# A graph kernel's count matrix: ScalarE's one-hots for two steps at once, a tile's normalization over several steps

## What is computed

```python
def _L0_gnn_ref(x, W_in, b_in, W_agg, W_self, b_hid, W_out, b_out, edge_index):
    ...
    h = x @ W_in + b_in
    deg = jax.ops.segment_sum(jnp.ones_like(dst, dtype=h.dtype), dst, num_segments=n)
    deg = jnp.maximum(deg, 1.0)[:, None]
    for l in range(n_layers):
        agg = jax.ops.segment_sum(h[src], dst, num_segments=n) / deg
        h = jax.nn.relu(agg @ W_agg[l] + h @ W_self[l] + b_hid[l])
    return h @ W_out + b_out
...
    edge_index = jnp.stack([src, dst])
    h = jnp.maximum(_layernorm(x, axis=-1), 0.0)
    x = x + _L0_gnn_ref(h, L0_gnn_W_in, L0_gnn_b_in, L0_gnn_W_agg, L0_gnn_W_self, L0_gnn_b_hid, L0_gnn_W_out, L0_gnn_b_out, edge_index)
```

## Time and profile before

| | us |
|---|---|
| median of 3 runs | 8374.22 |
| lowest, highest | 8368.79, 8376.52 |
| the profiled execution | 8375.02 |
| its span | 8373.1 |

### The profile page before, as it was taken

How to read it: one execution, slowest core, us unless ns; L and a number is a source line. 1 busy time by engine, 2 the same in 40 slices (tenths; PEclk the granted TensorE clock), 3 DMA queues, 4 the chain that set the end, 5 groups by cost and what they waited for, 6 DMA issues and landing times.

```text
span 8373.1 us, 125097 instructions
## 1 busy us (share of the span) xinstructions
PE 6630.0 (79%) x29456; PEld 4904.3 (59%) x29457; DVE 3788.5 (45%) x11036; ACT 2673.4 (32%) x7377; POOL 2390.8 (29%) x3589
## 2 busy tenths in 40 slices
PE   1666666669999999999688886479989996766766
PEld 0222222238887877777455554368778885666665
DVE  4888888851111111222477777512222333444443
ACT  0888888850000000111122221312223333222222
POOL 1111111110001001111577774000011114666664
PEclk9888888879999999999688887789999997888888
DMA  3444444467788778777233333388887773333332
GB/s 86 160 168 160 163 165 162 166 231 279 274 313 286 276 275 325 256 251 248 76 106 106 106 106 96 120 308 298 294 323 247 245 244 97 104 103 102 102 104 75
DMA packets 661157, 1591.43 MB, mean 190 GB/s; under 512 B 84103, under 2 KB 299160, under 8 KB 660825
## 3 DMA queue, kind: packets, MB, share of 16 engines
q1 hardware_dynamic: 534441, 1221.78, 41.1%
q0 software_dynamic: 126512, 366.84, 14.9%
HBM read 1199.09 MB, written 395.63 MB: 190 GB/s over the span
## 4 chain that ended last, share of the span: by engine, by line
PE 36%; issue 4%; DVEq 4%; DVE 4%; DMA 2%; ACT 1%; POOL 0%; SPq 0%; ACTq 0%; POOLq 0%
PE psum L1071 12%; PE psum L1211 6%; PE psum L1307 5%; PE psum L1277 3%; DVEq L2038 3%; PE psum L1199 2%; PE psum L1187 1%; PE psum L1289 1%; PE psum L1031 1%; PE psum L943 1%; PE psum L1040 1%; DMA slab<-adj 1%; DMA g_own<-own_dram 1%; DMA rb<-res 1%; PE psum L948 1%
## 5 line engine op out<-in xcount | busy, mean ns | idle before, releaser
L1071 PE MATMUL psum<-X,slab 128*128 128x512 f32 x12495 | 3115.2, 403 | 172.9 <-DMA slab<-adj 137.8
L1071 PEld LDWEIGHTS psum<-X,slab 128*128 128x128 f32 x12495 | 2350.7, 191 | 711.1 <-DMA slab<-adj 120.5
L1151 PE MATMUL psum<-hot_j,hot_key 128*128 128x392 bf16 x2348 | 692.3, 382 | 508.5 <-ACT hot_key L1409 426.6
L2035 DVE TENSOR_TENSOR acc<-acc,psum 128x264 f32 (+1 forms) x1660 | 699.6, 421 | 665.1 <-PE psum L1307 397.0
L1391 ACT ACTIVATE key_sq<-iota_row,edge_key 128x128 f32<-128x128 f32 x2348 | 813.7, 394 | 120.4 <-DVE staged L1859 2.3
L1914 DVE SCALAR_TENSOR_TENSOR staged<-staged,keep_all,psum 128x392 fp32r<-128x392 f32 x1174 | 727.3, 620 | 258.4 <-PE psum L1151 226.5
L1151 PEld LDWEIGHTS psum<-hot_j,hot_key 128*128 128x128 bf16 x2348 | 155.0, 102 | 987.0 <-ACT hot_key L1409 782.9
L794 POOL DMA_DIRECT2D table<-s_tab x147 | 80.2, 546 | 2048.8 <-DVE s_tab L1882 2048.8
L763 POOL TENSOR_TENSOR ends_fold<-fold,ends_all 128x16 fp32r<-128x16 f32 x1174 | 269.0, 229 | 1351.5 <-PE psum L1161 1328.3
L1161 PE MATMUL psum<-staged,ends_fold 128*16 128x392 f32 x1174 | 649.8, 553 | 0.5 <-DVE staged L1914 0.4
L1899 DVE TENSOR_SCALAR hot_j<-iota_j,edge_col 128x392 bf16<-128x392 bf16 x2348 | 643.2, 316 | 3.4
(11 more groups left out here) (351 smaller groups left out, 8374.6 us busy)
## 6 DMA issues: line engine op xcount, KB each, us to landing
slab<-adj SPq DMA_DIRECT2D x385, 1344.0 KB, 6.3
slab<-adj SPq DMA_DIRECT2D x315, 896.0 KB, 5.7
adj<-staged SPq DMA_DIRECT2D x1174, 196.0 KB, 1.9
X<-table SPq DMA_DIRECT2D x35, 1792.0 KB, 14.3
table<-s_tab POOLq DMA_DIRECT2D x147, 256.0 KB, 2.8
g_own<-own_dram POOLq DMA_DIRECT2D x35, 896.0 KB, 8.1
own_dram<-s_out POOLq DMA_DIRECT2D x147, 128.0 KB, 5.2
table<-s_tab SPq DMA_DIRECT2D x49, 256.0 KB, 2.1
```

The source lines that it names most:

```text
L1071: last = nc.tensor.matmul(sums_of(j), slab[:, c % SLABS, u, j * P:(j + 1) * P], X[:, d, :], start=(d == 0), stop=(d == KT - 1))
L1151: last = nc.tensor.matmul(psum[:, s % 4, 0:J], hot_key[:, s % 4, h, :], hot_j[:, s % 4, h, :], start=(h == 0), stop=(h == 1))
L2035: V.tensor_tensor(a, a, psum[:, bank, 0:w], ALU.add).then_inc(sem("summed"), 1)
```

## The change

ScalarE works in pairs of steps. `key_squares(t, m)` issues the four squares of steps 2m and 2m + 1 into one of three buffers, and one instruction of 512 columns writes `hot_key` of both steps into one of four buffers of two steps each. The squares of pair m + 1 now wait for the `hot_key` of pair m - 2, not for the instruction just ahead of them. `hot_key` of pair m waits for the product of step 2m - 7.

The stages get other places. VectorE: statistics at step 0, their merging (`in_moments`) at 1, the variance (`in_variance`) at 2, the reciprocal (`in_scale`) at 6, `nmr` (`in_shift`) at 7, `in_h0` at 12 (was 8), `in_rows` at 20 (was 15); the three waits for an own result that `then` made turn into waits one step later. ScalarE, in pairs: `in_sd` at pair 2, step 4 (was step 1), `in_h` at pair 4, step 8 (was 3), the copies at pairs 5 and 8, steps 10 and 16 (were 5 and 11), `in_hi` at pair 9, step 18 (was 13). TensorE: T1, P1, T2, P2 with P3 at 8, 10, 14, 16 (were 4, 6, 10, 12). SyncE: the load of the next tile at 10 (was 9), the tile's stores at 21 (was 20).

```diff
-                hot_key = sb("hot_key", [P, 4, 2, P], BF16, scope=late)
+                hot_key = sb("hot_key", [P, 4, 2, 2, P], BF16, scope=late)
...
-                key_sq = sb("key_sq", [P, 2, 2, P], scope=late)
+                key_sq = sb("key_sq", [P, 3, 2, 2, P], scope=late)
...
-                    if s == 9 and not (isinstance(t, int) and t == T - 1):
+                    if s == 10 and not (isinstance(t, int) and t == T - 1):
...
-                    if s == 20:
+                    if s == 21:
...
-                stages = {4: in_T1, 6: in_P1, 10: in_T2, 12: in_P2}
+                stages = {8: in_T1, 10: in_P1, 14: in_T2, 16: in_P2}
...
-                    pe.wait_ge(*ev("hot_key", t * BUILD + (s + 1)))
+                    pe.wait_ge(*ev("hot_key", t * (BUILD // 2) + (s // 2 + 1)))
...
-            def key_squares(t, s):
-
-                for h in range(2):
-                    last = nc.scalar.activation(key_sq[:, s % 2, h, :], iota_row[:], ACT.Square, bias=edge_key[:, h, bass.ds(t * BUILD + s, 1)],
-                                                scale=-1.0)
+            def key_squares(t, m):
+
+                for s in range(2 * m, 2 * m + 2):
+                    for h in range(2):
+                        last = nc.scalar.activation(key_sq[:, m % 3, s % 2, h, :], iota_row[:], ACT.Square,
+                                                    bias=edge_key[:, h, bass.ds(t * BUILD + s, 1)], scale=-1.0)
                 last.then_inc(sem("key_sq"), 1)
 
             def build(t, steps):
-                stages = {1: in_sd, 3: in_h, 5: taken_T("in", "T1", PS2_IN, ("P3", 1)), 11: taken_T("in", "T2", PS2_IN, ("P1", 2)), 13: in_hi}
-                for s in range(steps):
-                    n, static = t * BUILD + s, isinstance(t, int)
-                    if s in stages:
-                        stages[s](t)
-                    if not static or n + 1 < MEETS:
-                        if not static or n >= 1:
-                            act.wait_ge(*ev("hot_key", n))
-                        key_squares(t, s + 1)
-
-                    act.wait_ge(*ev("key_sq", t * BUILD + (s + 1)))
+                stages = {2: in_sd, 4: in_h, 5: taken_T("in", "T1", PS2_IN, ("P3", 1)), 8: taken_T("in", "T2", PS2_IN, ("P1", 2)), 9: in_hi}
+                for m in range(steps // 2):
+                    n, static = t * (BUILD // 2) + m, isinstance(t, int)
+                    if m in stages:
+                        stages[m](t)
+                    if not static or n + 1 < MEETS // 2:
+                        if not static or n >= 2:
+                            act.wait_ge(*ev("hot_key", t * (BUILD // 2) + (m - 1)))
+                        key_squares(t, m + 1)
+
+                    act.wait_ge(*ev("key_sq", t * (BUILD // 2) + (m + 1)))
                     if not static or n >= 4:
-                        act.wait_ge(*ev("meet_mm", t * BUILD + (s - 3)))
-                    nc.scalar.activation(hot_key[:, s % 4, :, :], key_sq[:, s % 2, :, :], ACT.Relu, bias=ones[:, 0:1], scale=-2.0).then_inc(sem("hot_key"), 1)
+                        act.wait_ge(*ev("meet_mm", t * BUILD + (2 * m - 6)))
+                    nc.scalar.activation(hot_key[:, m % 4, :, :, :], key_sq[:, m % 3, :, :, :], ACT.Relu, bias=ones[:, 0:1],
+                                         scale=-2.0).then_inc(sem("hot_key"), 1)
...
             def in_stats(t):
                 dve.wait_ge(*ev("in_x", t * 16 + 16))
                 V.memset(carrier[:, 6:7], 0.0)
-                then(V.bn_stats(st[:, 0, :], s_res[:, 0, :]), "in_st", t + 2)
+                V.bn_stats(st[:, 0, :], s_res[:, 0, :]).then_inc(sem("in_st"), 1)
+
+            def in_moments(t):
+                dve.wait_ge(*ev("in_st", t + 2))
                 V.memset(carrier[:, 6:7], 0.0)
-                then(V.bn_aggr(mv[:, 0, :], st[:, 0, :]), "in_mv", t + 2)
+                V.bn_aggr(mv[:, 0, :], st[:, 0, :]).then_inc(sem("in_mv"), 1)
+
+            def in_variance(t):
+                dve.wait_ge(*ev("in_mv", t + 2))
                 V.tensor_scalar_add(mv[:, 0, 1:2], mv[:, 0, 1:2], LN_EPS).then_inc(sem("in_ve"), 1)
 
-            def in_norm(t):
+            def in_scale(t):
                 dve.wait_ge(*ev("in_sd", t + 2))
-                then(V.reciprocal(rstd[:, 0:1], sd[:, 0:1]), "in_rstd", t + 2)
+                V.reciprocal(rstd[:, 0:1], sd[:, 0:1]).then_inc(sem("in_rstd"), 1)
+
+            def in_shift(t):
+                dve.wait_ge(*ev("in_rstd", t + 2))
...
-                stages = {0: in_stats, 2: in_norm, 8: in_h0, 15: in_rows}
+                stages = {0: in_stats, 1: in_moments, 2: in_variance, 6: in_scale, 7: in_shift, 12: in_h0, 20: in_rows}
```

More of the change, by code:

```diff
@@ L525, in build @@
         BUILD = 24
-        assert BUILD % AT_ONCE == 0 and (T - 1) * BUILD <= MEETS <= T * BUILD
+        assert BUILD % AT_ONCE == 0 and BUILD % 6 == 0 and MEETS % 2 == 0 and (T - 1) * BUILD <= MEETS <= T * BUILD
         def by_meets(eng, turn):
@@ L1150, in build @@
                     for h in range(2):
-                        last = nc.tensor.matmul(psum[:, s % 4, 0:J], hot_key[:, s % 4, h, :], hot_j[:, s % 4, h, :], start=(h == 0), stop=(h == 1))
+                        last = nc.tensor.matmul(psum[:, s % 4, 0:J], hot_key[:, s // 2 % 4, s % 2, h, :], hot_j[:, s % 4, h, :], start=(h == 0), stop=(h == 1))
                     last.then_inc(sem("meet_mm"), 1)
```

## The result

The changed kernel takes **8222.3 us** (median; 8214.1 to 8230.6), the kernel before 8373.1 us in the same comparison (8368.8 to 8376.5). The ratio is 0.982, with a 95% interval of 0.9803 to 0.9837. That is 151 us less. The prediction said 8240 us, 8160 to 8330, and faster with a chance of 0.91: it was right, 18 us too high.

The account below looks back on a forecast made before the run. ScalarE at 1.22 us a step heads the chain in the build; then VectorE's 25.9 us plus waits 0.39, 1.85, 0.3 and three quarters of 2.0 make 29.9 a tile, 2.75 less, times 48.9 = 134 us: 8240 us, range 8160 to 8330.

Parts of the forecast that it names:

- ScalarE's pace: A pair of steps on ScalarE costs 1.81 us (1.60 to 2.00), so ScalarE stops being the pace.
- Rival (4): Pairing does not free ScalarE, a pair costing 2.6 us: 8374 us stays; chance 0.03, shared with a balance of both.
- VectorE's own work: 24.0 us of steps plus 1.87 of stage operations, 25.9 us a tile; spreading the stages saves 0.36.
- Wait B: VectorE at step 8, as ScalarE's `in_h` waits for `nmr` from step 7: 1.85 us a tile, 0.36 more at low clock.
- three quarters: Share taken of the 2.0 us a tile that a low clock from Wait B until P1 would add.
- Wait A: VectorE at step 4, as ScalarE's `in_sd` waits for `in_variance` from step 2: 0.39 us a tile.
- Wait C: VectorE at step 10, behind P1 on TensorE: 1.63 us at the low clock, nothing at the high one.
- Wait D: VectorE at step 16, as P2 and P3 hold TensorE for 1.73 us: 0.3 us a tile.
- The sum: A build tile takes 28.4 us at high clock, 30.4 with it low until P1; 29.9 taken, 134 us less in all.
- Rival (1): The clock does not fall in Wait B: 28.4 us a tile, 8166 us; chance 0.18 for 8150 to 8200.
- Rival (2): The clock falls in every tile, back by P1's end: 30.4 us a tile, 8264 us; chance 0.64 together with the forecast.
- Rival (3): The clock stays low far beyond P1 and TensorE becomes the bound: 35.8 us a tile, 8529 us; chance 0.06.

Follow-up runs that it names:

- The fastest version: Changed kernel with VectorE's reciprocal at step 5, `nmr` at 6, bias at 14, ScalarE's stages one pair later, TensorE's two steps later: 8050.0 us, ratio 0.9615.
- waits filled: Changed kernel plus matmul products nobody reads on TensorE at step 4 and around T1 at step 8: ratio 0.9758 to the kernel before, tile 28.18 us.

## Why the prediction was right

**ScalarE's pace.** Right: a pair costs 1.78 us (1.81 predicted), `hot_key` 0.71 (0.70), its time on the engine 0.61 or 0.62 (0.61, by the copies of the earlier trace rows). Rival (4), that pairing frees nothing, is refuted by that.

**VectorE's own work.** The sum was near, two of its terms were not. In the changed kernel the statistics lengthen a step by 0.33 us (the `staged` at 1117.76 and 1119.09), `in_moments` and `in_variance` by 0.07 and 0.06, the reciprocal by 0.06 and `nmr` by 0.07. That is 0.59 for what was 1.21, so the spreading saves 0.62 us of work in this tile and not 3 x 0.12 = 0.36; it lies above the bound of 0.5. The term was made from the start of one small operation to the start of the next (0.46 where 0.34 would do), and left out that the next full operation, `hot_j`, is also held back after the last of a chain (1122.63 to 1122.85 is 0.22, and 0.06 now). With three additions of 0.33 the own work is 24.0 + 0.59 + 1.0 = 25.6 us and not 25.9. The fastest version, which hardly waits, shows it directly: 25.81 less 12.5/48.9 = 0.26 is 25.55.

**Wait B** was sized rightly. 1.85 was predicted at the high level, and the one filled with products is 1.82; 1.85 + 0.36 was predicted at the low one, and it is 2.08. That it is *the* new cost, and comes from where `nmr` stands, was shown by moving that line: 2.6 us a tile, C included. Over the 49 tiles its mean is 1.94 us, for the 1.85 and three quarters of 0.36, 2.12, that the sum of the prediction holds.

**Wait A** was 0.39 at the high level; it is 0.26 there (waits filled) and 0.60 in the tile shown, 0.43 in the mean. What the prediction missed is that the clock falls in A too: ScalarE's 2.76 us before `sd` leave TensorE 1.67 us idle. The sentence that ScalarE's waits are "harmless except behind B" is thereby wrong. With B gone and A left the tile takes 26.81 us and the clock is 0.91; with both gone 25.81 and 1.00.

**Wait C** was over-sized, 1.63 against 1.12 in the tile shown and 1.14 in the mean of the 37 tiles that have it. The step of TensorE at the low level was taken as 1.15 us. But those 1.15 were the rhythm of the keys, which ScalarE then made one every 1.22 us. In the trace of the kernel before, the key of the second of these steps ends at 1124.75 + 0.49 = 1125.24, and the weight load that needs it has waited 0.70 us for it:

```profile
1124.75 0.49 ACT L1409 ACTIVATE hot_key<-key_sq,ones 128x256 bf16<-128x256 f32 x1
...
1125.30 0.13 PEld L1151 LDWEIGHTS psum<-hot_j,hot_key 128*128 128x128 bf16 x2 [0.70 <-ACT hot_key L1409]
```

It is not what TensorE needs: with the keys ready it makes a step every 0.97 us (1122.93 to 1123.90) and 1.00 (1123.90 to 1124.90). The 0.90 from 1129.20 to 1130.10 are partly at the high level, which the clock left in that step (0.65 in 1129 to 1130). The Trainium skill, "TensorE: Matmul & The Clock Gate", Part 1, gives columns divided by 1.2 GHz from start to start while the array is cold; three products of 392 columns are by that an estimated 0.98 us a step, and the trace agrees with 0.97 and 1.00. The matmul of the degrees counts as one of the three: it leaves 1174 records for 1174 steps, so the two records for each instruction on 32-bit data, of which the part ahead of the prediction speaks, hold for P1 to P3 and not for it. A pitch measured on an engine that waits for another is the other's pitch.

**Wait D** was 0.3; in the tile before the one shown it is 0.30, and 0.29 in the mean.

**The sum.** Waits of 0.39 + 1.85 + 0.3 and three quarters of 2.0 make 4.0 us; measured are 174.6/48.9 = 3.6. Own work 25.9; measured 29.39 - 3.57 = 25.8 (a little of the waits, which overlap the end of the operation ahead, is in that). So 29.9 for 29.4, and 134 us for the build's 160, of which 151 are left between the medians. The forecast lay above on both terms, by some tenths each. The reason for the three quarters held, since 12 of the 49 tiles have no C; but no row gave the share, and that it came out at 37 of 49 is luck. C makes up most of what the waits were forecast too long: three quarters of 1.63 are 1.22 us a tile, and its mean is 0.86.

**The rivals.** Rival (1), 8166, would have been 28.4 us a tile; made with the filler products it is 28.2. Rival (2), 30.4, had its mechanism right, since the clock is at the low level at some time in all 49 tiles, though over P1 only in some three quarters of them, and its size too large by C. The rule of the same page of the Trainium skill that speaks for it, that the throttled level is the default, held in direction: the average tile (29.4) lies nearer to (2) as it now works out, 30.4 less 0.5 for C, than to (1). Rival (3), slower with TensorE as the bound, was far off for the reason given under C as well: a low step of 0.97 to 1.00 is no slower than VectorE's 1.00, so TensorE does not become the bound of the plain steps. By the prediction's own sum a whole tile at the low level would be 24 x 1.00 + 1.7 + 3.4 + 0.8 + 2.3 = 32.2 us, still less than 32.66. The 6 in 100 given to it rest on the mis-read 1.15.

What the prediction did not ask is which part of the change earns the gain. The pairs alone do all of it: a tile of 28.91 us against 29.39. Spreading the stages saves VectorE 0.6 us a tile and then loses it, by putting `nmr` at step 7, one step ahead of the pair that is held back for it. It stood at step 2, and at step 5 the same kernel takes 26.81.

## What to carry to other kernels

When an engine that feeds others is made faster, look next at the waits that stand in its program order: they are met sooner, swallow the lead, and set a pace of their own. Give what it waits for to an early step of the engine that makes it, ask for it late, and leave room between the two; an earlier `mv` alone brought nothing, since the next wait took up the lead. All the moves together were worth 171 us (8220.7 to 8050.0), more than the whole change (150 in the same comparison). Where a step's time at a low clock is wanted, take it where the engine is fed, and not where it waits.
